# Rows gathered by DMA, counts in f16, integers read from low halves: one change to a two-layer encoder kernel

## The chip, the cores and the metric

The kernel runs on one core of a Trainium2 chip. The metric is the device time of a whole execution in microseconds. The kernel before takes 1705.83 us (median of 3 runs, 1701.89 to 1706.07).

The engines are called TensorE (PE in the profile, its weight loads PEld), VectorE (DVE), ScalarE (ACT), GpSimd (POOL) and SyncE (SP, which here only issues transfers).

## The reference

Input is x, 128 sequences of 64 rows of 128 numbers, and a context of the same shape. Each of the four layers adds its result to x:

```
x = x + corr_attention(layernorm(x), ctx)     # correlation by Fourier transform, 4 best shifts
x = x + ffn(layernorm(x))                     # rows quantised to 8 bit, ternary weights
x = x + cross_attention(ctx, layernorm(x))    # 16 heads of 64, a sequence's 64 rows of x ask 64 + 64 rows
x = x + experts(layernorm(x))                 # router: softmax, 2 of 8 experts a row
```

Of these, the change touches the quantisation in ffn, with `q = clip(round(x * scale), -128, 127)` before both of its products; the layer norm of both the context and the twice-normed x ahead of cross attention; the router's count of rows per expert; and the last sum, `output + y * combine_w`.

## The kernel before

The 8192 rows are 64 tiles of 128 (two sequences each), in 16 groups of 4. x stays in SBUF from the first load to the last store. The stages follow each other, with a barrier between: weights, a first loop (both layers of layer 0), cross attention with the router, the experts, the combination.

The first loop goes over the groups, software-pipelined five deep: one pass holds group g's correlation, g-1's shifts, g-2's statistics and quantisation, g-3's first product and activation, g-4's second product. The order on each engine is written out by hand in `step`. `quantise` (L531) scales rows and adds 12582912 (ROUND), which leaves the rounded integer in the f32's low bits, subtracts it again into a bf16 tile (L541), and TensorE turns that with an identity (`turn_rows`, L743). `quantise_hidden` (L582) does the same with the 512 hidden numbers a row (L589, L592), turned in `turn_hidden` (L837). ScalarE copies what was turned out of PSUM (L647, L675).

Cross attention takes steps; a chunk is 4 heads of one tile, 256 in all, and a tile is 4 steps. The offsets (`AT_S = 3`: a step works on the scores of the chunk three ahead) set which step of the pipeline an operation belongs to, and the order of the `if`s in each engine's `step` sets its place within it. Each tile is brought in by two transfers of the context (L992, L993), with statistics (L1088, L1089), a power of minus a half on GpSimd (L1011), the normalisation (L1100, L1101), and GpSimd's gains and offsets (L1015 to L1022). In the tile kv, half of the partitions take rows of x and the other half rows of the context, at two places n = 0, 1: so the normalisation runs on 64 partitions at a time. The output of a tile is added to x in L1063, after which TensorE may overwrite its bank (L1284).

The router goes over groups in the same steps: a group's parts stand at the steps in `ROUTE_...` (L966 to 969), 16 steps to a group. It writes each row twice as a pair of f16 parts (L1218 on ScalarE, L1031 on GpSimd) behind the number of the row (L1127), once per chosen expert, and scatters them by indirect DMA (L1042). `r_xn` and `r_rows` are single buffers: L1107 waits for the rests of the group before (`row_done`), L1218 and L1127 wait for its scatters. The rank of a row in its expert comes from five f32 products with a triangle and with ones (L1309 to 1312).

The experts read tiles of 256 rows, and scatter the results by the row number into `z`, choice by choice, tile by tile. The combination reads z in two transfers a group (L1511), with pieces of 512 bytes, does eight multiply-adds on VectorE (L1527) and stores from ScalarE's queue.

Of the kernel before, what the change touches and what calls it, by code (L numbers as in the profile page):

```python
# [35 lines left out]
def constants():  # L36
# [30 lines left out]
    out[:, C_DST:C_DST + 2 * TILES] = np.arange(2 * TILES)[None] * P + ch[:, None]  # L67
# [6 lines left out]
    out[0, C_N0:C_N0 + 8] = np.arange(8) * BATCH * SEQ  # L74
# [43 lines left out]
def load_weights(nc, s, dram):  # L118
# [148 lines left out]
def first_layer(nc, s, dram):  # L267
# [10 lines left out]
    with ExitStack() as ctx:  # L278
# [32 lines left out]
        xr = sb("b_xr", [P, GT, D])  # L311
        qb = [sb(f"b_q{n}", [P, GT, D], BF16) for n in range(2)]
# [12 lines left out]
        q2 = [sb(f"b_q2{n}", [P, GT, FF], BF16) for n in range(2)]  # L325
# [142 lines left out]
        def _(dve):  # L468
# [62 lines left out]
            def quantise(g, k):  # L531
# [50 lines left out]
            def quantise_hidden(g, k):  # L582
# [54 lines left out]
        def _(act):  # L637
# [28 lines left out]
            def step(i, k):  # L666
# [66 lines left out]
        def _(pe):  # L733
            wq, wk, wv, wo = (s.w_l0[:, n, :] for n in range(4))

            def turn_rows(i, k, g, p):
# [5 lines left out]
                for j in range(GT):  # L742
                    pe.transpose(QT[:, P * j:P * j + P], qb[p][:, j, :], s.ident_b[:])  # L743
# [860 lines left out]
```

## Time and profile before

| | us |
|---|---|
| median of the runs | 1705.83 |
| profiled execution | 1701.37 |
| its span | 1699.5 |
| TensorE busy | 1416.6 (83%) |
| VectorE busy | 1433.0 (84%) |
| ScalarE busy | 1256.2 (74%) |
| GpSimd busy | 1087.7 (64%) |

The busy times are of one profiled execution, and its span is the time from its first instruction to its last. A wait is the idle time of an engine ahead of an instruction, with the instruction that released it. A line's number is that of the kernel before.

### The profile page before, as it was taken

Reading aid. Unit: us, or ns where it says so; the run is one execution under the profiler, and the core shown is the slowest. Engines: PE = TensorE matmul, PEld = TensorE weight load, DVE = VectorE, ACT = ScalarE, POOL = GpSimd, SP = SyncE. Lnnn points to the kernel's source line nnn. Section 1 sums busy time; section 2 is a strip of 40 time slices with the busy share of each in tenths; the row PEclk is TensorE's granted clock in tenths of the full one; section 3 lists DMA queues with packets and bytes.
Section 4 is the critical chain, followed back from the end, with each engine's and each line's share of the span. In section 5 each row is a group of like instructions: output and inputs, shape, how many; then the busy total and the mean of one; then the engine's idle time right before and its main releaser. Section 6 shows DMA issues by size and latency. Waiting matters only on the chain. (4 is left out here: it accounts for less than half of the span.)

```text
span 1699.5 us, 53032 instructions
## 1 busy us (share of the span) xinstructions
PE 1416.6 (83%) x17149; PEld 1211.3 (71%) x17165; DVE 1433.0 (84%) x4161; ACT 1256.2 (74%) x3802; POOL 1087.7 (64%) x1498
## 2 busy tenths in 40 slices
PE   4788888873899999999999999999999937999960
PEld 3676676752788787788778778877877726888850
DVE  3579999985899999999999999999999835888868
ACT  1368877763899999888889888888988805666640
POOL 1367776653656677786777778777777564666650
PEclk8989999986999999999999999999999968999985
DMA  4445444200000000000000000000000003332219
GB/s 138 162 164 182 172 162 154 105 1 8 8 8 7 7 18 15 11 17 12 11 16 16 12 11 15 14 11 14 16 11 8 13 32 81 86 83 79 81 29 297
DMA packets 101785, 97.22 MB, mean 57 GB/s; under 512 B 13256, under 2 KB 87275, under 8 KB 101504
## 3 DMA queue, kind: packets, MB, share of 16 engines
q1 hardware_dynamic: 84544, 74.22, 13.7%
q0 software_dynamic: 8640, 16.87, 3.0%
q10 hardware_dynamic: 8448, 4.20, 0.8%
q8 instruction: 83, 1.36, 0.3%
q14 instruction: 70, 0.57, 0.1%
HBM read 39.32 MB, written 56.83 MB: 57 GB/s over the span
## 5 line engine op out<-in xcount | busy, mean ns | idle before, releaser
L1002 POOL TENSOR_TENSOR c_p<-c_p,c_rden 128x512 f32<-128x512 f32 x256 | 266.4, 1040 | 174.1 <-DVE c_rden L1067 172.1
L1207 ACT ACTIVATE c_p<-bank,c_nmax 128x128 f32<-128x128 f32 x1024 | 361.6, 375 | 4.7 <-DVE c_nmax L1053 4.6
L1207 ACT ACTIVATION_READ_ACCUMULATOR c_p<-bank,c_nmax 128x1 f32 x1024 | 221.6, 216 | 0.0
L1378 POOL DMA_INDIRECT moe_outputs<-e_y,e_rows x142 | 151.8, 1069 | 94.1 <-DVE e_y L1407 58.5
L1053 DVE TENSOR_REDUCE c_nmax<-bank 128x4 f32<-128x512 f32 x256 | 174.2, 681 | 38.1 <-PE bank L109 34.3
L107 PE MATMUL bank<-c_kvT,qk_fused 128*128 128x128 f16 x1024 | 187.6, 221 | 1.6 <-ACT c_kvT L1186 1.4
L108 PE MATMUL bank<-c_kvT,qk_fused 128*128 128x128 f16 x1024 | 187.5, 221 | 0.0
L109 PE MATMUL bank<-c_kvT,qk_fused 128*128 128x128 f16 x1024 | 187.5, 221 | 0.0
L1274 PE MATMUL bank<-const,c_p 128*128 128x128 f32 x1024 | 156.8, 276 | 13.3 <-DVE c_pT0rest L1078 12.4
L1446 ACT ACTIVATE e_h<-bank,moe_b 128x256 f32<-128x256 f32 x284 | 117.8, 465 | 65.0 <-PE bank L109 63.6
L1042 POOL DMA_INDIRECT moe_slots<-r_rows,r_pos x128 | 131.0, 1023 | 35.8 <-issue 35.8
L107 PE MATMUL bank<-vo_fused,c_o0high 128*128 128x128 f16 x512 | 93.2, 220 | 32.2 <-DVE x L1063 32.2
L1274 PEld LDWEIGHTS bank<-const,c_p 128*128 128x128 f32 x1024 | 108.3, 141 | 15.9 <-POOL c_p L1002 13.2
L107 PE MATMUL bank<-vo_fused,c_o1high 128*128 128x128 f16 x512 | 92.6, 220 | 19.5 <-DVE x L1063 19.5
L107 PEld LDWEIGHTS bank<-c_kvT,qk_fused 128*128 128x128 f16 x1024 | 103.4, 101 | 3.3 <-ACT c_kvT L1186 2.3
L1191 ACT ACTIVATE c_pT0high<-bank 128x512 f16<-128x512 f32 x128 | 76.7, 599 | 34.4 <-PE bank L1274 33.8
L108 PEld LDWEIGHTS bank<-c_kvT,qk_fused 128*128 128x128 f16 x1024 | 101.3, 99 | 0.4
L109 PEld LDWEIGHTS bank<-c_kvT,qk_fused 128*128 128x128 f16 x1024 | 101.3, 99 | 0.0
L107 PE MATMUL bank<-c_kvT,c_g0high 128*128 128x128 f16 x512 | 93.8, 221 | 1.4 <-DVE c_g0rest L1072 1.3
L1072 DVE SCALAR_TENSOR_TENSOR c_g0rest<-bank,c_g0high 128x512 f16<-128x512 f32 x128 | 84.9, 663 | 11.2 <-ACT c_g0high L1181 11.2
L108 PE MATMUL bank<-c_kvT,c_g0high 128*128 128x128 f16 x512 | 93.8, 221 | 0.0
L109 PE MATMUL bank<-c_kvT,c_g0rest 128*128 128x128 f16 x512 | 93.7, 221 | 0.0
(312 smaller groups left out, 6006.1 us busy)
## 6 DMA issues: line engine op xcount, KB each, us to landing
moe_slots<-slot_fill SPq DMA_DIRECT2D x66, 516.0 KB, 5.7
e_rows<-moe_slots SPq DMA_DIRECT2D x71, 129.0 KB, 2.2
f_z<-moe_outputs SPq DMA_DIRECT2D x32, 256.0 KB, 4.9
x<-in_x SPq DMA_DIRECT2D x16, 256.0 KB, 3.2
a_ctx<-in_ctx SPq DMA_DIRECT2D x32, 128.0 KB, 3.3
moe_stage<-in_L_ffn_W SPq DMA_DIRECT2D x16, 256.0 KB, 3.1
c_ctx<-in_ctx SPq DMA_DIRECT2D x128, 32.0 KB, 2.0
out_x<-x ACTq DMA_DIRECT2D x16, 256.0 KB, 4.8
```

Of the source, the lines that this page charges most:

```text
L107: pe.matmul(out, lhs[0], rhs[0], start=start, stop=False)
L108: pe.matmul(out, lhs[0], rhs[1], start=False, stop=False)
L109: return pe.matmul(out, lhs[1], rhs[0], start=False, stop=stop)
L1002: pool.tensor_tensor(pr[r % 4][:], pr[r % 4][:], rep(rden[r % 4][:], 2, P), ALU.mult).then_inc(m["pn"], 1)
L1042: pool.indirect_dma_start(s.xs, bass.IndirectOffsetOnAxis(ap=pos[:, c, j:j + 1], axis=0), rows[:, c, j, :], None).then_inc(scattered, 16)
L1053: dve.tensor_reduce(nmax[r % 4][:], SB[r % 2][:].rearrange("p (h c) -> p h c", h=4), AX.X, ALU.max, negate=True).then_inc(m["max"], 1)
L1072: dve.scalar_tensor_tensor(lo, GB[r % 2][:].rearrange("p (a n) -> p a n", a=2), 0.125, hi, ALU.mult, ALU.subtract).then_inc(m["g_copied"], 1)
L1191: act.activation(ptc[r % 2][0][:], PT[:], ACT.Copy).then_inc(m["pt_high"], 1)
L1207: last = act.activation(pr[r % 4][:, h, :], SB[r % 2][:, P * h:P * h + P], ACT.Exp, bias=nmax[r % 4][:, h:h + 1], accum_out=den[r % 4][:, ...
L1274: last = pe.transpose(PT[:, P * h:P * h + P], pr[r % 4][:, h, :], s.ident)
L1378: pool.indirect_dma_start(s.z, bass.IndirectOffsetOnAxis(ap=xr[t % XBUF][:, h, 2 * D:ROW].bitcast(U32), axis=0), ys[t % YBUF][:, h, :], No ...
L1446: act.activation(hf[t % 2][:, b, :], HB[b][:, 0:TSLOT], ACT.Gelu_apprx_tanh, bias=s.moe_b1[:, bass.ds(e * KB + b, 1)]).then_inc(m["gelu"], 1)
```

## The change

It has six parts.

1. First loop: ROUND_HALF = ROUND + 0x6600 is added instead of ROUND. The low 16 bits of the f32 are then, read as f16, the number 1536 + q. TensorE turns these halves at once (every second f16 of the f32 tile), and ScalarE takes 1536 off as it copies. The two subtractions on VectorE go. ScalarE's copy of 640 columns becomes two, since the last 128 are bf16 still.
2. Cross attention: a tile `c_rows` of two places takes the place of `c_ctx`. Four transfers a tile bring rows of the context from memory, and rows of x from SBUF, to the place and the half where the normalisation wants them; it then works on 128 partitions at a time. GpSimd does the epsilon in two operations with a drain between.
3. The addition of the output (L1063, L1072 after) goes to the head of VectorE's step, ahead of the maximum.
4. The router's mask, counts, triangle and ones are f16. Copies of rows, rests and row numbers move by one step.
5. The rows of z are numbered by partition first, then tile, then choice: a partition's results are then side by side.
6. Combination: two transfers a group, pieces of 2 KB. ScalarE scales the second choice, VectorE does four multiply-adds and one addition of 512.

```diff
-                for j in range(GT):
-                    dve.tensor_scalar(xr[:, j, :], xc[:, j, :], qs[:, j:j + 1], ROUND, ALU.mult, ALU.add)
-                dve.drain()
                 wait(dve, mb["qt"], g - 1)
-                dve.tensor_scalar(qb[k][:], xr[:], ROUND, None, ALU.subtract).then_inc(mb["q"], 1)
+                for j in range(GT):
+                    last = dve.tensor_scalar(xr[k][:, j, :], xc[:, j, :], qs[:, j:j + 1], ROUND_HALF, ALU.mult, ALU.add)
+                last.then_inc(mb["q"], 1)
...
-                    dve.tensor_scalar(ge[k][:, j, :], ge[k][:, j, :], qs2[:, j:j + 1], ROUND, ALU.mult, ALU.add)
-                dve.drain()
-                wait(dve, mb["q2t"], 2 * (g - 1))
-                dve.tensor_scalar(q2[k][:], ge[k][:], ROUND, None, ALU.subtract).then_inc(mb["q2"], 1)
+                    last = dve.tensor_scalar(ge[k][:, j, :], ge[k][:, j, :], qs2[:, j:j + 1], ROUND_HALF, ALU.mult, ALU.add)
+                last.then_inc(mb["q2"], 1)
...
+        def integers(ap, first):
+
+            return ap.bitcast(F16)[:, 2 * first:2 * (first + P):2]
...
-                        last = pe.transpose(T2[r][:, to:to + P], q2[p][:, 2 * r + j, P * b:P * b + P], s.ident_b[:])
+                        last = pe.transpose(T2[r][:, to:to + P], integers(ge[p][:, 2 * r + j, :], P * b), s.ident_h[:])
...
-                    act.activation(qt[b[1]][:], QT[:, 0:GT * P + P], ACT.Copy).then_inc(mb["qt_copied"], 1)
+                    act.activation(qt[b[1]][:, 0:GT * P], QT[:, 0:GT * P], ACT.Identity, bias=s.moffset[:])
+                    act.activation(qt[b[1]][:, GT * P:GT * P + P], PT[:, GT * P:GT * P + P], ACT.Copy).then_inc(mb["qt_copied"], 1)
...
-        ROUTE_HIGH, ROUTE_LOW, ROUTE_STEP, ROUTE_BASE, ROUTE_POS = 43, 44, 44, 46, 47
+        ROUTE_HIGH, ROUTE_LOW, ROUTE_STEP, ROUTE_BASE, ROUTE_POS = 44, 45, 45, 46, 47
...
-                sp.dma_start(cs[k][0:64, :], cvw[1, t, :, :]).then_inc(c_loaded[k], 16)
-                sp.dma_start(cs[k][64:128, :], cvw[0, t, :, :]).then_inc(c_loaded[k], 16)
+                for half in range(2):
+                    rows = slice(64 * half, 64 * half + 64)
+                    sp.dma_start(cs[k][rows, 1 - half, :], cvw[1 - half, t, :, :]).then_inc(c_loaded[k], 16)
+                    sp.dma_start(cs[k][rows, half, :], s.xg(i)[rows, k, :]).then_inc(c_loaded[k], 16)
...
-                    for half in range(2):
-                        rows = slice(64 * half, 64 * half + 64)
-                        dve.tensor_scalar(kv[r][rows, half, :], s.xg(g)[rows, r, :], a[rows, 0, 0:1], b[rows, 0:1], ALU.subtract, ALU.mult)
-                        last = dve.tensor_scalar(kv[r][rows, 1 - half, :], cs[r][rows, :], a[rows, 1, 0:1], b[rows, 1:2], ALU.subtract, ALU.mult)
+                    for n in range(2):
+                        last = dve.tensor_scalar(kv[r][:, n, :], cs[r][:, n, :], a[:, n, 0:1], b[:, n:n + 1], ALU.subtract, ALU.mult)
...
-    zv = s.z.rearrange("(k t p) d -> p k t d", k=2, p=P)
+    zv = s.z.rearrange("(p t k) d -> p t k d", k=2, p=P)
...
+                for j in range(GT):
+                    last = act.activation(share[g % 2][:, j, :], zt[g % 4][:, j, 1, :], ACT.Copy, scale=gate[:, GT * g + j, 1:2])
+                last.then_inc(m["scaled"], 1)
...
-                for k in range(2):
-                    for j in range(GT):
-                        last = dve.scalar_tensor_tensor(s.xg(g)[:, j, :], zt[q][:, k, j, :], gate[:, GT * g + j, k:k + 1], s.xg(g)[:, j, :], ALU.mult, ALU.add)
-                    if k == 0:
-                        dve.drain()
-                last.then_inc(m["combined"], 1)
+                for j in range(GT):
+                    dve.scalar_tensor_tensor(s.xg(g)[:, j, :], zt[g % 4][:, j, 0, :], gate[:, GT * g + j, 0:1], s.xg(g)[:, j, :], ALU.mult, ALU.add)
+                dve.drain()
+                dve.wait_ge(m["scaled"], g + 1)
+                dve.tensor_tensor(s.xg(g), s.xg(g), share[g % 2][:], ALU.add).then_inc(m["combined"], 1)
```

VectorE in the middle of one pass of the first loop, before and then after (`b_q` is the bf16 tile of integers, `b_gelu` the hidden numbers, in the second piece lines are numbered as in the changed kernel):

```order
L584 RECIPROCAL b_qs<-b_mx 128x4 [waits b_scale2]
L586 SCALAR_TENSOR_TENSOR b_qs<-b_qs,b_tmp 128x4
L589 TENSOR_SCALAR b_gelu<-b_gelu,b_qs 128x512 x4
L592 TENSOR_SCALAR b_q<-b_gelu 128x2048
L483 TENSOR_TENSOR a_prod<-bank,a_kk 128x512 [waits a_kk_copied]
L533 RECIPROCAL b_qs<-b_mx 128x4 [waits b_r1]
L535 SCALAR_TENSOR_TENSOR b_qs<-b_qs,b_rr 128x4
L538 TENSOR_SCALAR b_xr<-b_xc,b_qs 128x128 x4
L541 TENSOR_SCALAR b_q<-b_xr 128x512 [waits b_qt]
```

```order
L592 RECIPROCAL b_qs<-b_mx 128x4 [waits b_scale2]
L594 SCALAR_TENSOR_TENSOR b_qs<-b_qs,b_tmp 128x4
L597 TENSOR_SCALAR b_gelu<-b_gelu,b_qs 128x512 x4
L492 TENSOR_TENSOR a_prod<-bank,a_kk 128x512 [waits a_kk_copied]
L542 RECIPROCAL b_qs<-b_mx 128x4 [waits b_r1]
L544 SCALAR_TENSOR_TENSOR b_qs<-b_qs,b_rr 128x4
L548 TENSOR_SCALAR b_xr<-b_xc,b_qs 128x128 [waits b_qt]
L548 TENSOR_SCALAR b_xr<-b_xc,b_qs 128x128 x3
```

The two rows that write `b_q` are gone, and `a_prod` and everything behind it follow at once on the scaling.

VectorE in cross attention, from a normalisation (`c_kv`) to the statistics of the next tile, before and then after:

```order
L1100 TENSOR_SCALAR c_kv<-x,c_mv,c_rstd 64x128 [waits c_kv,c_rstd]
L1101 TENSOR_SCALAR c_kv<-c_ctx,c_mv,c_rstd 64x128
L1100 TENSOR_SCALAR c_kv<-x,c_mv,c_rstd 64x128
L1101 TENSOR_SCALAR c_kv<-c_ctx,c_mv,c_rstd 64x128
L1127 TENSOR_SCALAR r_rows<-r_rows 128x8 [waits r_scattered]
L1053 TENSOR_REDUCE c_nmax<-bank 128x4 [waits c_s]
L1063 TENSOR_TENSOR x<-x,bank 128x128 [waits c_w]
L1067 RECIPROCAL c_rden<-c_den 128x4 [waits c_exp]
L1072 SCALAR_TENSOR_TENSOR c_g0rest<-bank,c_g0high 128x2x256 [waits c_g_high]
L1078 TENSOR_TENSOR c_pT1rest<-bank,c_pT1high 128x512 [waits c_pt_high]
L1084 TENSOR_TENSOR c_o1rest<-bank,c_o1high 128x8x64 [waits c_o_high]
L1088 BN_STATS c_bn<-x 128x6 [waits c_ctx_loaded3]
```

```order
L1118 TENSOR_SCALAR c_kv<-c_rows,c_mv,c_rstd 128x128 [waits c_kv,c_rstd]
L1118 TENSOR_SCALAR c_kv<-c_rows,c_mv,c_rstd 128x128
L1072 TENSOR_TENSOR x<-x,bank 128x128 [waits c_w]
L1076 TENSOR_REDUCE c_nmax<-bank 128x4 [waits c_s]
L1086 RECIPROCAL c_rden<-c_den 128x4 [waits c_exp]
L1091 SCALAR_TENSOR_TENSOR c_g0rest<-bank,c_g0high 128x2x256 [waits c_g_high]
L1097 TENSOR_TENSOR c_pT1rest<-bank,c_pT1high 128x512 [waits c_pt_high]
L1103 TENSOR_TENSOR c_o1rest<-bank,c_o1high 128x8x64 [waits c_o_high]
L1108 BN_STATS c_bn<-c_rows 128x6 [waits c_ctx_loaded3]
```

The four rows of 64 partitions are two of 128. The addition to x (L1063) stood behind the maximum (`c_nmax`) and now stands ahead of it, and the row numbers (`r_rows`) have moved behind the statistics.

GpSimd around the rests of the router's rows (`r_rows<-r_xn`), where `c_p<-c_p,c_rden` is the first operation of each step, before and then after:

```order
L1031 TENSOR_TENSOR r_rows<-r_xn,r_rows 128x4x128 [waits r_row_high]
L1031 TENSOR_TENSOR r_rows<-r_xn,r_rows 128x4x128
L1002 TENSOR_TENSOR c_p<-c_p,c_rden 128x512 [waits c_rden]
L1015 TENSOR_TENSOR c_kv<-c_kv,ln_g 128x256 [waits c_kvn]
L102 ISA
L1018 TENSOR_TENSOR c_kv_parts<-c_kv,ln_b 128x256 [waits c_o]
L1020 TENSOR_TENSOR c_kv<-c_kv,ln_b 128x256
L1022 TENSOR_TENSOR c_kv_parts<-c_kv,c_kv_parts 128x256
L1002 TENSOR_TENSOR c_p<-c_p,c_rden 128x512 [waits c_rden]
```

```order
L1013 TENSOR_TENSOR c_p<-c_p,c_rden 128x512 [waits c_rden]
L1027 TENSOR_TENSOR c_kv<-c_kv,ln_g 128x256 [waits c_kvn]
L107 ISA
L1030 TENSOR_TENSOR c_kv_parts<-c_kv,ln_b 128x256 [waits c_o]
L1032 TENSOR_TENSOR c_kv<-c_kv,ln_b 128x256
L1034 TENSOR_TENSOR c_kv_parts<-c_kv,c_kv_parts 128x256
L1043 TENSOR_TENSOR r_rows<-r_xn,r_rows 128x4x128 [waits r_row_high]
L1043 TENSOR_TENSOR r_rows<-r_xn,r_rows 128x4x128
L1013 TENSOR_TENSOR c_p<-c_p,c_rden 128x512 [waits c_rden]
```

The rests stood in a step of their own, right behind a `c_p`; now they stand one step later, behind the four rows of `c_kv`.

## Rows read from the trace of the kernel before

**Rows 1.** Three stages: busy us per engine, granted clock, DMA share, GB/s.

```profile
85.00:412.00 327.00, 260.21 (x2353) 212.22 (x2369) 287.15 (x1101) 240.45 (x475) 215.38 (x398) 0.94 0.34 122
412.00:1392.00 980.00, 880.45 (x11634) 758.78 (x11633) 874.72 (x2410) 836.57 (x2930) 691.22 (x917) 0.97 0.04 13
1656.00:1699.50 43.50, 0.00 (x0) 0.00 (x0) 35.20 (x128) 0.00 (x0) 0.00 (x0) 0.50 0.99 290
```

**Rows 2.** Waits, 412 to 1392 us: total us, times, longest.

```profile
PE bank L107 <- DVE x L1063: 51.8, 61, 2.3
DVE c_nmax L1053 <- PE bank L109: 34.3, 60, 1.3
ACT r_rows L1218 <- DMA moe_slots<-r_rows,r_pos: 34.0, 14, 11.4
```

**Rows 3.** Combination, 1645 to 1700 us, and two windows with DMA rates.

```profile
L1527 DVE SCALAR_TENSOR_TENSOR x<-f_z,d_gate,x 128x128 f32<-128x128 f32 x128 | 35.2, 345 | 13.1 <-DMA f_z<-moe_outputs 11.8
...
75.00:80.00 5.00, 2.89 (x24) 2.51 (x22) 4.60 (x12) 1.67 (x3) 0.00 (x0) 1.00 1.04 404
1676.00:1680.00 4.00, 0.00 (x0) 0.00 (x0) 3.85 (x15) 0.00 (x0) 0.00 (x0) 0.50 1.15 345
```

**Rows 4.** Groups by shape, 100 to 340 us; the last row from the page.

```profile
L837 PE MATMUL bank<-ident_bf,b_q 128*128 128x128 bf16 x176 | 13.5, 220 | 12.5 <-DVE b_q L592 12.5
L592 DVE TENSOR_SCALAR b_q<-b_gelu 128x2048 bf16<-128x2048 f32 x11 | 13.5, 1227 | 1.2 <-issue 0.6
...
L541 DVE TENSOR_SCALAR b_q<-b_xr 128x512 bf16<-128x512 f32 x12 | 5.1, 427 | 0.9
...
L1274 PE MATMUL bank<-const,c_p 128*128 128x128 f32 x1024 | 156.8, 276 | 13.3 <-DVE c_pT0rest L1078 12.4
```

**Rows 5.** One group of the first loop in time, VectorE, then ScalarE.

```profile
226.06 0.69 DVE L483 TENSOR_TENSOR a_prod<-bank,a_kk 128x512 f32<-128x512 f32 x1
...
237.64 1.10 DVE L490 MAX8 a_top<-a_corr 128x8 f32<-128x64 f32 x8
...
240.39 0.17 DVE L494 TENSOR_TENSOR a_ev<-a_top 128x32 f32<-128x32 f32 x1
...
246.15 0.68 DVE L483 TENSOR_TENSOR a_prod<-bank,a_kk 128x512 f32<-128x512 f32 x1
...
235.16 0.60 ACT L719 ACTIVATE a_corr<-bank 128x512 f32<-128x512 f32 x1 [0.31 <-PE bank L809]
...
240.86 0.70 ACT L675 ACTIVATE b_qt<-bank 128x640 bf16<-128x640 bf16 x1
...
245.53 0.58 ACT L652 ACTIVATE a_kk<-bank 128x512 f32<-128x512 f32 x1
```

**Rows 6.** Groups by shape, 400 to 1360 us: busy us, mean ns, idle before.

```profile
L1207 ACT ACTIVATE c_p<-bank,c_nmax 128x128 f32<-128x128 f32 x1024 | 361.6, 375 | 4.7 <-DVE c_nmax L1053 4.6
...
L1101 DVE TENSOR_SCALAR c_kv<-c_ctx,c_mv,c_rstd 64x128 f32<-64x128 f32 x128 | 45.3, 354 | 0.0
...
L1100 DVE TENSOR_SCALAR c_kv<-x,c_mv,c_rstd 64x128 f32 x88 | 38.5, 437 | 0.7
...
L1100 DVE TENSOR_SCALAR c_kv<-x,c_mv,c_rstd 64x128 f32<-64x128 f32 x40 | 14.5, 363 | 6.0 <-POOL c_rstd L1011 5.7
```

**Rows 7.** VectorE in order of time, cross attention: start us, us, line.

```profile
823.98 0.98 DVE L1100 TENSOR_SCALAR c_kv<-x,c_mv,c_rstd 64x128 f32 x1
824.89 0.33 DVE L1101 TENSOR_SCALAR c_kv<-c_ctx,c_mv,c_rstd 64x128 f32<-64x128 f32 x1
...
831.76 1.54 DVE L1107 TENSOR_SCALAR r_xn<-x,r_mv,r_rstd 128x128 f32 x4
```

**Rows 8.** GpSimd in order of time, the steps of rows 7.

```profile
822.70 2.19 POOL L1031 TENSOR_TENSOR r_rows<-r_xn,r_rows 128x512 f16<-128x512 f32 x2
827.01 1.04 POOL L1002 TENSOR_TENSOR c_p<-c_p,c_rden 128x512 f32<-128x512 f32 x1 [2.13 <-DVE c_rden L1067]
...
830.78 0.68 POOL L1022 TENSOR_TENSOR c_kv_parts<-c_kv,c_kv_parts 128x256 f16<-128x256 f32 x1
```

More of the change, by code:

```diff
@@ L66, in constants @@
     out[:, C_ONE:C_ONE + P] = 1
-    out[:, C_DST:C_DST + 2 * TILES] = np.arange(2 * TILES)[None] * P + ch[:, None]
+    choice, tile = np.arange(2)[:, None], np.arange(TILES)[None, :]
+    out[:, C_DST:C_DST + 2 * TILES] = (2 * (ch[:, None, None] * TILES + tile) + choice).reshape(P, 2 * TILES)
     out[:, C_IT:C_IT + 72] = np.arange(72)[None]
@@ L73, in constants @@
         out[:, C_TILE + j] = ch // 32 == j
-    out[0, C_N0:C_N0 + 8] = np.arange(8) * BATCH * SEQ
+    out[:, C_N0:C_N0 + 8] = np.arange(8)[None] * (BATCH * SEQ // P)
     return out.astype(np.float32)
@@ L310, in first_layer @@
         xc = sb("b_xc", [P, GT, D])
-        xr = sb("b_xr", [P, GT, D])
-        qb = [sb(f"b_q{n}", [P, GT, D], BF16) for n in range(2)]
+        xr = [sb(f"b_xr{n}", [P, GT, D]) for n in range(2)]
         qt = [sb(f"b_qt{n}", [P, GT * P + P], BF16) for n in range(2)]
@@ L557, in bias_rows @@
             def bias_rows():
-                hi, mid, lo, all_ = (q2[0][:, n, :] for n in range(4))
+                hi, mid, lo, all_ = (ge[1][:, n // 2, :].bitcast(BF16)[:, n % 2 * FF:n % 2 * FF + FF] for n in range(4))
                 rest = ge[0][:, 0, :]
@@ L656, in gelu @@
                 if j == 0:
-                    wait(act, mb["q2"], g - 1)
+                    wait(act, mb["q2t"], 2 * (g - 1))
                 act.activation(ge[k][:, j, :], HB[j % 2][:], ACT.Gelu, scale=deq[k][:, j:j + 1]).then_inc(mb["gelu"], 1)
@@ L905, in cross_attention @@
         parts = lambda name, shape: [sb(name + part, shape, F16) for part in ("high", "rest")]
-        cs = [sb(f"c_ctx{n}", [P, D]) for n in range(4)]
+        cs = [sb(f"c_rows{n}", [P, 2, D]) for n in range(4)]
         kv = [sb(f"c_kv{n}", [P, 2, D]) for n in range(4)]
@@ L1007, in step @@
                     pool.wait_ge(m["stats"], v + 1)
-                    pool.tensor_tensor(b[:, 1:2], a[:, 1, 1:2], s.eps[:, 0:1], ALU.add)
-                    pool.tensor_scalar(b[:, 0:1], a[:, 0, 1:2], 1.0 + EPS, EPS * EPS, ALU.mult, ALU.add)
+                    pool.tensor_tensor(b[:], a[:, :, 1], norm_mul[:], ALU.mult)
+                    pool.drain()
+                    pool.tensor_tensor(b[:], b[:], norm_add[:], ALU.add)
                     pool.drain()
@@ L1043, in step @@
                                             rows[:, c, j, :], None).then_inc(scattered, 16)
+            for half in range(2):
+                rows_of = slice(64 * half, 64 * half + 64)
+                pool.memset(norm_mul[rows_of, half:half + 1], 1.0 + EPS)
+                pool.memset(norm_mul[rows_of, 1 - half:2 - half], 1.0)
+                pool.memset(norm_add[rows_of, half:half + 1], EPS * EPS)
+                pool.memset(norm_add[rows_of, 1 - half:2 - half], EPS)
+            pool.drain()
             walk(pool, FIRST, LAST, 16, LO, HI, step)
@@ L1049, in step @@
             def step(i, k):
+                if t := tile(i, k, AT_X3):
+                    v, r, g = t
+                    dve.wait_ge(m["w"], 4 * v + 4)
+                    dve.tensor_tensor(s.xg(g)[:, r, :], s.xg(g)[:, r, :], WB[:, 0:P], ALU.add).then_inc(m["x3"], 1)
                 if n := number(i, k, AT_S, CHUNKS):
@@ L1086, in step @@
                     v, r, g = t
-                    dve.wait_ge(c_loaded[r], 32 * (g + 1))
-                    dve.bn_stats(bst[:, 0, :], s.xg(g)[:, r, :])
-                    dve.bn_stats(bst[:, 1, :], cs[r][:])
+                    dve.wait_ge(c_loaded[r], 64 * (g + 1))
+                    for b in range(2):
+                        dve.bn_stats(bst[:, b, :], cs[r][:, b, :])
                     dve.drain()
@@ L1136, in step @@
                     dve.tensor_tensor(crun[:], crun[:], picked[:], ALU.add)
-            dve.tensor_scalar(dest, s.dst_rows.rearrange("p (k t) -> p k t", k=2)[:, :, 0:GT], float(-GT * P), None, ALU.add)
+            dve.tensor_scalar(dest, s.dst_rows.rearrange("p (k t) -> p k t", k=2)[:, :, 0:GT], float(-2 * GT), None, ALU.add)
             dve.tensor_copy(crun[:], s.count0)
+            dve.tensor_copy(tri[:], s.tri)
+            dve.tensor_copy(ones[:], s.ones)
             dve.memset(one8[:], 1.0)
@@ L1497, in combine @@
 def combine(nc, s, m, z_in, sb, gate, out):
-    zt = [sb(f"f_z{n}", [P, 2, GT, D]) for n in range(4)]
+    zt = [sb(f"f_z{n}", [P, GT, 2, D]) for n in range(4)]
+    share = [sb(f"f_share{n}", [P, GT, D]) for n in range(2)]
     ov = out.rearrange("(t two) s d -> (two s) t d", two=2)
-    zv = s.z.rearrange("(k t p) d -> p k t d", k=2, p=P)
+    zv = s.z.rearrange("(p t k) d -> p t k d", k=2, p=P)
     with nc.Block() as block:
```

56 lines of the change are left out of this document (32 added, 24 removed).

## The prediction

> **What bounds the kernel now.** I read the stages first, then who waits for whom in the longest stage, then the costliest groups of instructions by shape, then the order of time of single groups. The stages [rows 1]: the first loop runs from 85 to 412 us, cross attention with the router from 412 to 1392, the combination from 1656 to the end; the experts between are not touched but for where their results are written. In the first loop VectorE is busy 287 of 327 us, in cross attention 875 of 980, beside ScalarE 837 and TensorE 880. So VectorE leads narrowly, and what is taken from it is worth less than its length, since two engines stand 4 to 5% behind. The waits of cross attention [rows 2] say the same: TensorE idles 51.8 us for the addition of the output (L1063), VectorE 34.3 us for scores from TensorE, ScalarE 34.0 us for the router's scatters. In the combination VectorE issues without a gap: 3.85 of 4 us, while the DMA moves 345 GB/s [rows 3].
>
> **First loop.** Removed are one subtraction of 128x512 (427 ns) and one of 128x2048 (1227 ns) in each of 16 groups [rows 4]. With the overlap of neighbours (some 0.09 us) and the drains (0.08 us) that went with them, both go at their length: 1.65 us a group, 26 us in all. A group takes 246.15 - 226.06 = 20.1 us [rows 5], and VectorE works 287 of the stage's 327 us, so it is VectorE's own length that counts. Two things take some back. ScalarE's copy of 128x640 (0.70 us) becomes one of 128x512 and one of 128x128. It stands in a chain that starts at VectorE's L494 (ends 240.56) and ends with L652 (245.53 + 0.58 = 246.11), and VectorE's product starts at 246.15, without slack [rows 5]. The second copy costs between 0.1 (the difference in width) and 0.6 us (a whole copy); I take 0.3, near the small ScalarE operations, which is 4 us over 13 full groups. And ScalarE has its correlation ready at 235.76, where VectorE, which takes it at 237.64 and is 1.65 shorter by then, will want it at 235.99 [rows 5]: 0.2 us of slack are left, and for the groups that miss it I take 2 us in all. The bias in the three copies hides in that same idle time of ScalarE; without cover it would be 0.1 us each, 5 us. So the first loop gives **-20 us** (bounds -26 and -10).
> The transposes of the integers will read every second f16: 20 a group, 320 in all, 0.22 us each now, where an f32 transpose of the same size takes 0.276 [rows 4]. Strided reading costs between nothing and that difference, 0.056 x 320 = 18 us if all of it were on the path; I take nothing, because the elements still number 128, and TensorE waited 12.5 us in 12 groups for the operation that goes [rows 4], which covers most of it.
>
> **Cross attention, normalisation.** Each of 64 tiles now has four VectorE operations on 64 partitions, 38.5 + 14.5 + 45.3 = 98.3 us together [rows 6]. After there are two a tile on 128 partitions with as many elements each. I price them as L1101, 354 ns: 128 x 0.354 = 45.3 us. Saved are 53 us, less the overlap with the neighbour that also goes (824.96 - 824.89 = 0.07 us [rows 7], 128 times, 9 us): 44 us. By L1107 (1.54 us for four, beside GpSimd [rows 7]) the new ones would cost 0.385 each and 40 us would be saved; I go between, 42. ScalarE and TensorE are close behind, so I let three quarters count: **-31** (bounds -44 and -15).
> **The output added first.** TensorE's product for the next tile waits for L1063, 51.8 us over 64 tiles, 0.8 us a tile. L1063 now goes ahead of the maximum (0.68 us). TensorE gains up to 0.7 us a tile, 43 us, but TensorE isn't the bound; what VectorE can get is a part of its 34.3 us of waits for scores [rows 2]. I take a quarter: **-8** (0 to -25).
> **The router one step later.** Row copies (ScalarE), rests (GpSimd) and row numbers (VectorE) each move one step. ScalarE's wait for the scatters, 34.0 us in 14 groups with one of 11.4 at the end, mostly goes in the loop: of 34.0 - 11.4 = 22.6 I let two thirds go, 15 us of ScalarE, worth **-6** (0 to -15). But GpSimd's rests (2.19 us) land behind the four operations of the layer norm in the same step, and VectorE's L1107 waits for them. In the trace the step's first GpSimd multiplication starts at 827.01, the four end at 831.46, and L1107 starts at 831.76 [rows 7, 8]. With the rests behind 831.45 they end at 833.64, so VectorE would stand still for 1.9 us a group, 15 times, 28 us. VectorE has a few waits in that step which would absorb part, and after a stall it finds the others ahead: I take **+18** (bounds +5 and +30). Queued behind L1107 on VectorE are the maximum of the next step and all that ScalarE's exponentials need. GpSimd's next multiplication comes 2.2 us late too, but TensorE reads it two steps (7.4 us) later.
> A collision goes: L1100 took 0.98 us at 823.98 and ended at 824.96, just as GpSimd's rests (822.70 + 2.19 = 824.89) ended, against a mean of 437 and 363 ns [rows 6, 7, 8]. After the change the rests don't lie beside the normalisation: 0.6 us x 14, of which I count **-6**. By the Trainium skill (SBUF — State Buffer, Who interferes with whom) VectorE's two-port operations and GpSimd exclude each other for a whole instruction. The row agrees; by the rule L1107, released together with GpSimd's next multiplication, could lose up to 1.0 us to it once more, which would be 15 us, though its 1.54 us for four already hold such a collision.
> The counts in f16 turn five f32 products of a group into single-pass ones, on TensorE, which isn't the bound: **-2** (0 to -8). The square root's extra multiplication with a drain on GpSimd (0.3 us a tile) is hidden by the two steps until its reader. The rows of x gathered by DMA add 128 small transfers of 32 KB; VectorE waits only at the first tile, where the SP queue issues four transfers instead of two: **+1** (0 to +2).
> Cross attention: -31 - 8 - 6 + 18 - 6 - 2 + 1 = **-34 us**.
>
> **Combination.** A group has 8 VectorE operations, 35.2/16 = 2.2 us, 2.27 with the drain [rows 3]. After there are 4 of them (1.1 us), a drain and one addition of 128x512 (0.69 us by L483, of the same size [rows 5]): 1.9 us, 0.37 less, 16 times 5.9 us. ScalarE's four scalings, at most 0.375 each by its exponentials [rows 6], make 1.5 us and lie beside. A group moves 0.79 MB, which in 1.9 us is 414 GB/s; the DMA reached 404 in another window [rows 3], so it is at its end: **-4** (bounds 0 and -6).
>
> **The sum.** -20 - 34 - 4 = -58 us. The profiled execution took 1701.4 us (span 1699.5 and 1.9 around it), which is 4.4 below the median shown, 1705.8. So the changed kernel stands at 1643 by the one and 1648 by the other; I forecast **1648 us**.
>
> **Rivals.** *The freed time turns into waits.* If ScalarE and TensorE hold the pace of cross attention, VectorE's 42 us are worth a third, the reordering nothing, and the stall at L1107 counts in full: -14 - 6 + 28 = +8 there, -20 and -4 beside it, 1690. For it: ScalarE is at 85% and TensorE at 90% of the stage; against it: the waits of VectorE are only 4% of the stage. A milder form, half of the whole sum, gives 1677.
> *Everything counts.* VectorE's whole saving and no stall: -26 - 42 - 15 - 10 - 5 = -98, 1608. Against it: the chain through L652 has no slack now.
> *Slower: the results lie apart.* The expert results of a partition lie 64 KB apart from the next one's, where before neighbours of 512 bytes lay side by side. If the memory serves that badly, the combination is bound by it: it moves 12.6 MB (36.4 us at 345 GB/s), and the change comes out slower than before once the rate falls under 12.6 MB / (36.4 + 58 us) = 133 GB/s; at 115 GB/s it takes 110 us, 1648 + 74 = 1722. For it nothing in the trace; against it 2 KB pieces in place of 512 bytes, and one fast window.
> [...]
> *The integers aren't cheaper.* If strided reading costs TensorE the full f32 price in the chain, the first loop gives -2 instead of -20: 1666.
>
> **How the numbers follow.** Forecast 0.52 (1628 to 1668 by itself), waits in place of work 0.24 (1690, or 1677 in the milder form), everything 0.08, integers dear 0.08, slower through the memory 0.05, something else 0.03. About 0.3%, 5 us, is what a measurement of this kernel tells from none. Within 5 us of before falls only the worst end of the second case, 0.04; slower is the memory and half of the rest, 0.06; faster 0.90. The range 1614 to 1694 leaves out the slower case and the outer part of "everything".
>
> **What would show it.** Right: the first loop shorter by about 20 us and its groups at 18.7 us with a wait of VectorE for L652; cross attention at about 946 us; a wait of VectorE's L1107 for GpSimd's rests of 1 to 2 us a group; TensorE's wait for the addition at a third; the combination at 39 us with more than 360 GB/s. Wrong: no shorter group in the first loop (then TensorE or the strided reads bind), ScalarE's or TensorE's waits unchanged in length while VectorE's grow, or transfers of the results landing later than now.

## The result, and the profile after

The changed kernel takes 1645.6 us (median of 3, 1640.1 to 1647.7) against 1705.8: ratio 0.9643, interval 0.9628 to 0.9657. Forecast were 1648. The profiled execution took 1647.7, its span is 1645.9, 53.6 us less than before (1699.5). I cut both traces at the same instructions: start +1.7, first loop -19.3, cross attention with the router -30.6, experts -1.3, combination -4.1.

The three stages, to be read against [rows 1] (same columns; windows moved with the stage):

```profile
86.66:394.36 307.70, 262.19 (x2370) 211.21 (x2370) 265.07 (x1069) 244.31 (x491) 214.69 (x398) 0.93 0.36 130
394.36:1343.55 949.19, 867.79 (x11553) 751.60 (x11551) 829.22 (x2284) 827.79 (x2930) 695.76 (x925) 0.96 0.06 18
1606.48:1645.90 39.42, 0.00 (x0) 0.00 (x0) 28.63 (x80) 20.44 (x64) 0.00 (x0) 0.50 0.95 320
```

VectorE lost 22 us of work in the first loop and 45 in cross attention, where the stage got only 31 shorter: it is now busy 829 of 949 us, a smaller share (87%) than before (89%), so something else holds it as well.

The first loop: one group in time, VectorE and then ScalarE (start us, length us), against [rows 5].

```profile
222.60 0.68 DVE L492 TENSOR_TENSOR a_prod<-bank,a_kk 128x512 f32<-128x512 f32 x1
...
232.73 1.10 DVE L499 MAX8 a_top<-a_corr 128x8 f32<-128x64 f32 x8
...
235.48 0.17 DVE L503 TENSOR_TENSOR a_ev<-a_top 128x32 f32<-128x32 f32 x1
...
240.48 0.86 DVE L481 BATCH_NORM_STATS2 a_bn<-x 128x6 f32 x4
241.39 0.69 DVE L492 TENSOR_TENSOR a_prod<-bank,a_kk 128x512 f32<-128x512 f32 x1
```

```profile
235.96 0.69 ACT L681 ACTIVATE b_qt<-bank,minus_offset 128x512 bf16<-128x512 f16 x1
236.55 0.27 ACT L682 ACTIVATE b_qt<-bank 128x128 bf16<-128x128 bf16 x1
...
240.78 0.58 ACT L658 ACTIVATE a_kk<-bank 128x512 f32<-128x512 f32 x1
```

A group takes 241.39 - 222.60 = 18.79 us, 1.30 less, and so it is over ten groups (19.1 us against 20.4). The chain from L503 to L658 and on to L492 has no slack in this group (240.78 + 0.58 = 241.36): from the start of L503 to the end of L658 it takes 5.88 us, against 5.72 from L494 to L652 before, 0.16 more, which is what the two copies take beyond the one (235.96 to 236.82, 0.86 us, against 0.70). But VectorE's own work ends with it (240.48 + 0.86 = 241.34). Of the eleven groups from 143 to 336 us only four wait for that copy; in the other seven it was there 0.1 to 1.0 us before, and VectorE's own work sets the pace. The transposes that read every second f16, to be read against [rows 4]:

```profile
L844 PE MATMUL bank<-ident_f,b_gelu 128*128 128x128 f16 x176 | 13.5, 220 | 0.1
```

Same count, same 220 ns, and the wait of 12.5 us in front of them is gone: the stride costs TensorE nothing.

The waits of cross attention after (engine, tile, line, and what was waited for: total us, times, longest), against [rows 2]:

```profile
DVE c_nmax L1076 <- PE bank L114: 37.2, 59, 1.2
ACT c_p L1226 <- DVE c_nmax L1076: 36.9, 28, 2.5
PE bank L1293 <- DVE c_pT1rest L1097: 36.5, 17, 2.7
...
DVE r_xn L1124 <- POOL r_rows L1043: 21.5, 14, 3.6
ACT r_rows L1237 <- DMA moe_slots<-r_rows,r_pos: 19.3, 2, 11.3
...
PEld bank L112 <- DVE x L1072: 6.7, 20, 1.1
...
PE bank L112 <- DVE x L1072: 0.9, 1, 0.9
```

TensorE's wait for the addition is all but gone (its products 0.9 us against 51.8, where a third was forecast), and so is ScalarE's for the scatters in the loop: the two that are left come at 1324 us and later. The stall that was forecast is there, 1.5 us a group at VectorE's L1124 (L1107 before), and two waits that I had not in the sum stand behind it: ScalarE for the maximum (4.6 us before), TensorE for L1097 (0.9 us for L1078 before). One group in time, VectorE, GpSimd, ScalarE and TensorE:

```profile
742.05 0.68 DVE L1103 TENSOR_TENSOR c_o1rest<-bank,c_o1high 128x512 f16<-128x512 f32 x1
744.19 1.64 DVE L1124 TENSOR_SCALAR r_xn<-x,r_mv,r_rstd 128x128 f32 x4 [1.46 <-POOL r_rows L1043]
...
746.20 0.66 DVE L1076 TENSOR_REDUCE c_nmax<-bank 128x4 f32<-128x512 f32 x1
...
741.77 2.20 POOL L1043 TENSOR_TENSOR r_rows<-r_xn,r_rows 128x512 f16<-128x512 f32 x2
743.94 1.04 POOL L1013 TENSOR_TENSOR c_p<-c_p,c_rden 128x512 f32<-128x512 f32 x1
...
746.89 0.37 ACT L1226 ACTIVATE c_p<-bank,c_nmax 128x128 f32<-128x128 f32 x1 [2.50 <-DVE c_nmax L1076]
...
748.40 0.72 PE L1293 MATMUL bank<-const,c_p 128*128 128x128 f32 x4 [2.70 <-DVE c_pT1rest L1097]
```

And the same place in windows of 2 us (columns as in [rows 1]; the third number from the end is the granted clock, 1.00 is 2.4 GHz and 0.50 is 1.2):

```profile
744.00:746.00 2.00, 1.70 (x31) 1.52 (x28) 1.81 (x5) 0.39 (x1) 1.72 (x4) 1.00 0.00 0
746.00:748.00 2.00, 0.00 (x0) 0.00 (x0) 1.93 (x7) 1.10 (x7) 1.24 (x2) 1.00 0.00 0
748.00:750.00 2.00, 1.60 (x7) 0.88 (x8) 1.68 (x6) 1.49 (x5) 0.20 (x1) 0.70 0.00 0
750.00:752.00 2.00, 2.00 (x19) 1.81 (x17) 2.00 (x5) 1.57 (x8) 1.40 (x3) 0.50 0.00 0
752.00:754.00 2.00, 2.00 (x30) 1.92 (x29) 1.24 (x5) 1.50 (x5) 1.07 (x1) 0.95 0.00 0
```

TensorE does nothing for 2.70 us, its clock then drops to half, and it works at half speed until about 752 us. From 575 us on the clock falls in nine of 13 groups, each time for about 3.4 us; cut into stretches of 15 us, the stage is short of 15.0 us of full clock.

### The profile page after: what moved, and what is told of

Read it like the earlier page. It is cut to its first block and busy times, and to the rows that moved or that the text cites. A ratio compares the mean times of both kernels' runs of the same rounds, so it can differ in the third digit from the quotient of the medians.

```text
span 1645.9 us, 52961 instructions
## 1 busy us (share of the span) xinstructions
PE 1407.7 (86%) x17084; PEld 1202.6 (73%) x17084; DVE 1359.9 (83%) x3955; ACT 1271.9 (77%) x3882; POOL 1091.5 (66%) x1507
## 5 line engine op out<-in xcount | busy, mean ns | idle before, releaser
L1226 ACT ACTIVATE c_p<-bank,c_nmax 128x128 f32<-128x128 f32 x1024 | 365.8, 388 | 37.0 <-DVE c_nmax L1076 36.9
L1013 POOL TENSOR_TENSOR c_p<-c_p,c_rden 128x512 f32<-128x512 f32 x256 | 266.8, 1042 | 134.6 <-DVE c_rden L1086 131.8
L1226 ACT ACTIVATION_READ_ACCUMULATOR c_p<-bank,c_nmax 128x1 f32 x1024 | 232.2, 228 | 0.0
L112 PE MATMUL bank<-c_kvT,qk_fused 128*128 128x128 f16 x1024 | 189.9, 223 | 4.3 <-ACT c_kvT L1205 3.6
L113 PE MATMUL bank<-c_kvT,qk_fused 128*128 128x128 f16 x1024 | 189.6, 222 | 0.0
L114 PE MATMUL bank<-c_kvT,qk_fused 128*128 128x128 f16 x1024 | 189.3, 222 | 0.0
L114 PE MATMUL bank<-vo_fused,c_o0rest 128*128 128x128 f16 x512 | 96.7, 225 | 0.0
L113 PE MATMUL bank<-vo_fused,c_o0high 128*128 128x128 f16 x512 | 96.6, 225 | 0.0
L112 PE MATMUL bank<-vo_fused,c_o0high 128*128 128x128 f16 x512 | 96.5, 225 | 0.0
L112 PE MATMUL bank<-c_kvT,c_g1high 128*128 128x128 f16 x512 | 93.5, 221 | 0.0
L113 PE MATMUL bank<-c_kvT,c_g1high 128*128 128x128 f16 x512 | 93.3, 220 | 0.0
L114 PE MATMUL bank<-c_kvT,c_g1rest 128*128 128x128 f16 x512 | 93.1, 220 | 0.0
```

Of the source, the lines that this page charges most:

```text
L112: pe.matmul(out, lhs[0], rhs[0], start=start, stop=False)
L113: pe.matmul(out, lhs[0], rhs[1], start=False, stop=False)
L114: return pe.matmul(out, lhs[1], rhs[0], start=False, stop=stop)
L1013: pool.tensor_tensor(pr[r % 4][:], pr[r % 4][:], rep(rden[r % 4][:], 2, P), ALU.mult).then_inc(m["pn"], 1)
L1226: last = act.activation(pr[r % 4][:, h, :], SB[r % 2][:, P * h:P * h + P], ACT.Exp, bias=nmax[r % 4][:, h:h + 1], accum_out=den[r % 4][:, ...
```

## The experiments

The second and third sets of runs met a chip on which the experts took 57 to 75 us longer for every kernel traced there, before included by its time (1768.9 and 1784.2 us); there I go by the ratio to before and by the length of cross attention in each trace, from VectorE's first preparation for the router (L1154) to its last table (L1188). A fall is one of the stretches of 3.4 us, in the middle of the stage, in which TensorE's clock is granted at half.

| kernel | ratio to before | interval | cross attention us | clock missing us | falls |
|---|---|---|---|---|---|
| before | 1 | | 982.9 | 4.9 | 3 |
| changed | 0.9643 | 0.9628-0.9657 | 952.3 | 15.0 | 9 |
| changed, again | 0.9645 | 0.9628-0.9662 | 949.3 | 13.2 | 8 |
| changed, third | 0.9691 | 0.9634-0.9747 | 965.5 | 18.4 | 11 |
| rests first | 0.9532 | 0.9516-0.9549 | 931.1 | 0 | 0 |
| router back | 0.9527 | 0.9510-0.9544 | 931.4 | 0 | 0 |
| addition behind | 0.9692 | 0.9677-0.9708 | 959.6 | 18.3 | 11 |
| first loop alone | 0.9875 | 0.9818-0.9933 | | | |
| norm in halves | 0.9837 | 0.9791-0.9883 | 977.2 | 10.0 | 6 |
| f32 counts | 0.9564 | 0.9517-0.9611 | 939.9 | 0 | 0 |
| f32 counts, again | 0.9527 | 0.9478-0.9575 | 939.9 | 0 | 0 |
| rests first, f32 | 0.9506 | 0.9445-0.9567 | 933.7 | 0 | 0 |
| rests first, spread | 0.9537 | 0.9485-0.9589 | 931.9 | 0 | 0 |
| results in 512 bytes | 0.9732 | 0.9675-0.9790 | 965.2 | 20.1 | 12 |

(Clock missing: the sum over stretches of 15 us from 435 to 1290 us of 15 x (1 - granted clock).)

**The base.** 

> The changed kernel once more, beside the kernels that it is compared with. Expected 0.964 of the time before, some 1645 us.

1644.9 us, as expected.

**The rests ahead of the layer norm.**

```diff
+                if (g := group(i, k, ROUTE_LOW)) is not None:      # moved here, unchanged
                 if t := tile(i, k, AT_KV):
...
-                if (g := group(i, k, ROUTE_LOW)) is not None:
```

> GpSimd's rests of the router's rows (L1043) go ahead of the four operations of the layer norm in the same step; nothing else is changed. Theory: VectorE's stall at L1124 (21.5 us in 14 groups) is on the path and pushes the maximum behind it, for which ScalarE then waits (36.9 us). Without it the wait at L1124 falls under 3 us, ScalarE's wait for the maximum to half, and cross attention gets 12 to 22 us shorter: 1623 to 1633 us. Rival: the stall is made good by work that stands ready behind it; then the wait goes and the time stays within 3 us of the changed kernel. Second rival: the layer norm, 2.2 us later on GpSimd, makes TensorE wait for the rows; then L1265's wait grows by 1 us or more a group and the time does not fall.

1626.7 us, 18.3 less than the changed kernel beside it. The stall is gone in the loop (one wait of 3.6 us at the start is left), and with it the falls of the clock. ScalarE's wait for the maximum fell by a third, not to half. The two rivals are out: L1265's only wait stays at 11.7 us.

**The router's rows back.**

```diff
-        ROUTE_HIGH, ROUTE_LOW, ROUTE_STEP, ROUTE_BASE, ROUTE_POS = 44, 45, 45, 46, 47
+        ROUTE_HIGH, ROUTE_LOW, ROUTE_STEP, ROUTE_BASE, ROUTE_POS = 43, 44, 44, 46, 47
```

> The router's row copies, rests and row numbers stand one step earlier again (43, 44, 44), the rest as in the changed kernel. Theory, by the terms forecast: the stall at L1124 goes (-18), the wait of ScalarE for the scatters (13 waits, 22.6 us before) comes back (+6), and the collision of GpSimd's rests with a normalisation (+6): 6 us less than the changed kernel, some 1639 us. Rival: the later step was worth more than its stall, since a waiting ScalarE holds everything; then the time is 8 us or more above the changed kernel.

1626.3 us, 18.6 less, where 6 were expected. Its waits in cross attention, and its normalisation:

```profile
ACT r_rows L1237 <- DMA moe_slots<-r_rows,r_pos: 35.0, 14, 11.3
...
ACT c_p L1226 <- DVE c_nmax L1076: 10.6, 16, 0.8
```

```profile
L1118 DVE TENSOR_SCALAR c_kv<-c_rows,c_mv,c_rstd 128x128 f32<-128x128 f32 x128 | 58.1, 494 | 5.5 <-POOL c_rstd L1023 5.5
```

and those of the version with the rests first:

```profile
ACT c_p L1226 <- DVE c_nmax L1076: 25.7, 26, 1.7
...
ACT r_rows L1237 <- DMA moe_slots<-r_rows,r_pos: 19.6, 2, 11.5
```

ScalarE waits 35.0 + 10.6 = 45.6 us in the one and 25.7 + 19.6 = 45.3 in the other. The wait for the scatters did not cost; taken away, it turned up as a wait for VectorE.

The collision of GpSimd's rests with the normalisation is real too: 494 ns a piece, against 374 in the changed kernel run beside it, 15 us in all. But these runs can't price it. With the rests first, L1124 meets GpSimd instead, and VectorE spends as long on the normalisation and L1124 together in either version: 58.1 + 22.3 = 80.4 us here, 47.9 + 32.7 = 80.6 with the rests first, against 42.6 + 25.1 = 67.7 in the changed kernel. Both versions took the stall away and brought 13 us of collisions back.

**The addition behind the maximum.** The four lines of L1072 go back to where L1063 was. 

> The addition of the output stands behind the maximum again, the rest as in the changed kernel. Theory: TensorE waits for it again, 30 to 50 us in all, and the time grows by 8 us (4 to 15): 1653 us. Rival: TensorE isn't the bound and ScalarE, which now waits 36.9 us for the maximum, gets it 0.2 us a tile earlier; then the time stays or falls by up to 5 us though TensorE's wait comes back.

1653.8 us, 8.9 more. The sum's term was 8. TensorE waits for the addition again, 31.8 us in its weight loads and 6.8 in its products, and the rival, no change or a gain, is out. A part of the 8.9 us is clock, since it falls in 11 groups here and in 8 of the changed kernel beside it.

**The first loop alone,** in the kernel before. 

> The kernel before with the first loop of the changed kernel and nothing else of it. Theory: the two operations go at their length less what ScalarE's chain gives back, 1.3 us a group (the changed kernel's group took 241.39 - 222.60 = 18.79 us, against 20.09): -20 us, some 1686 us, cross attention, experts and combination as before. Rival: the first loop's gain seen in the changed kernel comes in part from elsewhere, or is lost in the next stage, which starts earlier; then the time stays above 1692 us.

Ratio 0.9875 (0.9818 to 0.9933), which on 1706 us is -21 (-31 to -11). It agrees and can't say more: the rival, above 1692 us, is only just inside the interval. Its traced execution, 1773 us, is one of the three longest of eight (1747 to 1775), so I take nothing from its trace.

**The normalisation in halves.**

```diff
-                    for n in range(2):
-                        last = dve.tensor_scalar(kv[r][:, n, :], cs[r][:, n, :], a[:, n, 0:1], b[:, n:n + 1], ALU.subtract, ALU.mult)
+                    for half in range(2):
+                        rows = slice(64 * half, 64 * half + 64)
...                      # two operations on these 64 rows
```

> The changed kernel with the normalisation by four operations on 64 partitions again, its inputs gathered by DMA as now. VectorE gets 128 operations more; by the means of the rows 50 to 56 us of work. Theory as forecast: three quarters of 42 us count, so 31 us above the changed kernel (15 to 44), 1676 us. Rival: ScalarE, which now waits 36.9 us for VectorE's maximum, was not that close behind, and all of it counts: 42 us or more above. Second rival: what was gained came from the stall's neighbours; under 15 us.

Against the changed kernel's 0.9645 and 0.9691 it is 1.5 to 1.9% of 1706, 25 to 33 us; with the intervals it is some 12 to 41 us. The theory holds and the first rival is out. The second, under 15 us, is unlikely but not out: cross attention took 977.2 us, 25 and 28 more than in the changed kernel's first two traces, but only 12 more than in its third, where the clock fell 11 times and not 6.

**The counts in f32.**

```diff
-        mask = sb("r_mask", [P, GT, EXPERTS], F16)
+        mask = sb("r_mask", [P, GT, EXPERTS])
...
-        tri, ones = sb("r_tri", [P, P], F16), sb("r_ones", [P, P], F16)
+        tri, ones = s.tri, s.ones
...                      # and the running count, in f32 too
```

> The changed kernel with the router's masks and counts in f32 again. Theory: TensorE gets about 1.5 us of work a group more, of which little is on the path: 0 to 4 us above the changed kernel, 1647 us. Rival: the ranks stand between the mask and VectorE's positions with no slack; then 8 us or more.

Neither of the two: cross attention took 939.9 us, 9 to 12 less than the changed kernel in its first two traces, though VectorE stands still as before (20.7 us in 14 waits). At the place shown above, TensorE now does this (its wait, then the clock around it):

```profile
745.83 0.63 PE L1291 MATMUL bank<-const,c_p 128*128 128x128 f32 x4 [1.75 <-DVE c_pT1rest L1097]
```

```profile
743.00:745.00 2.00, 1.08 (x20) 0.91 (x17) 1.93 (x8) 0.67 (x4) 1.20 (x2) 1.00 0.00 0
745.00:747.00 2.00, 1.17 (x8) 0.73 (x9) 1.69 (x6) 1.75 (x8) 0.63 (x1) 1.00 0.00 0
747.00:749.00 2.00, 2.00 (x37) 2.00 (x36) 1.99 (x5) 1.97 (x9) 1.13 (x2) 1.00 0.00 0
```

The longer products fill TensorE just ahead of the stall, it idles 1.75 us instead of 2.70, and the clock stays. So I ran it again beside the changed kernel, and both edits together. 

> The changed kernel beside the next three. In its trace TensorE idles 2.70 us once in most groups of cross attention (until VectorE's L1097 behind the stall), and the clock granted to it is 0.70 and 0.50 in the 4 us behind that. Expected 0.9645 of the time before.

> The f32 counts once more, now beside the changed kernel. In the first run cross attention took 939.9 us against 949 to 952, and no stretch of 15 us of it had a clock under 1.00 from 420 us on. Theory from that: the f32 products fill 1 us a group of TensorE beside the stall, its longest idle time is 1.8 us in place of 2.7, the clock stays at its full level, and this is worth 8 to 12 us, more than the products cost: 1634 us, ratio to before 0.958. Rival: the first run's gain was a disturbance; then the time is 0 to 4 us above the changed kernel.

> The rests ahead of the layer norm and the f32 counts together. Theory: the two gains are the same one in part, since without the stall no clock is lost; then f32 counts are worth nothing on top or cost up to 4 us: 1626 to 1631 us, ratio 0.953 to 0.956. Rival: the gains are independent and add, -18 and -10: 1617 us, ratio 0.948.

The changed kernel came to 0.9691 here, with the expected 0.9645 inside its interval, the f32 counts to 0.9527, and both edits together to 0.9506, where 0.953 to 0.956 was expected and the rival's 0.948 can't be told from it; its trace (933.7 us) stands with the theory.

The intervals of the changed kernel (0.9634 to 0.9747) and of the f32 counts (0.9478 to 0.9575) don't meet, and the stage is 939.9 us both times: the disturbance is out. Of the four combinations, by cross attention: stall and f16 949 to 966, stall and f32 939.9, no stall and f32 933.7, no stall and f16 931.1. So the stall alone costs 6.2 us and f16 alone gains 2.6, but the two together cost 18 to 34. The gains are the same one in part, as expected; whole times can't tell the last two from each other.

That the rest is clock can be read inside one trace. These are three groups of the changed kernel, each from one L1124 to the next (columns as in [rows 1]), and TensorE's long wait in each:

```profile
801.50:858.90 57.40, 54.41 (x726) 47.53 (x723) 51.53 (x143) 51.71 (x184) 44.24 (x59) 0.97 0.06 18
858.90:914.70 55.80, 52.80 (x725) 45.71 (x722) 51.99 (x143) 51.39 (x184) 44.28 (x59) 1.00 0.06 19
914.70:972.10 57.40, 54.40 (x725) 47.09 (x723) 51.50 (x143) 51.67 (x184) 44.22 (x59) 0.97 0.06 18
```

```profile
805.71 0.63 PE L1293 MATMUL bank<-const,c_p 128*128 128x128 f32 x4 [2.69 <-DVE c_pT1rest L1097]
...
863.06 0.63 PE L1293 MATMUL bank<-const,c_p 128*128 128x128 f32 x4 [2.70 <-DVE c_pT1rest L1097]
...
918.88 0.63 PE L1293 MATMUL bank<-const,c_p 128*128 128x128 f32 x4 [2.70 <-DVE c_pT1rest L1097]
```

The code, the stall and the idle time are the same in all three. Where the clock fell, the group took 57.4 us, and where it did not, 55.8. From 687 to 1256 us this trace has seven groups of the first kind (57.1 to 57.4 us) and three of the second; in the same part of the stage every group takes 55.7 to 55.9 us with f32 counts, and 55.3 or 55.4 with the rests first. A fall costs 1.5 us, then, and the nine of them some 14; the stall without a fall costs 0.5 us a group. In the third trace a fall costs more, 2.2 us (58.1 us on average against 55.9); why stays open.

**The router's scalings spread over four steps,** with the rests first.

```diff
-                    for j in range(GT):
-                        last = dve.tensor_scalar(r_xn[:, j, :], ...
+                for j in range(GT):
+                    if (g := group(i, k, ROUTE_XN + j)) is not None:
```

> A version meant to beat both: GpSimd's rests ahead of the layer norm, and VectorE's four router scalings (L1124, 1.3 to 2.4 us in one step, behind which ScalarE waits 25.7 us for the maximum) spread over four steps, one in each. Theory: ScalarE's wait for the maximum falls to a third or less and 5 to 12 us go: 1615 to 1622 us. Rival: VectorE is the bound over the whole of a tile, and an order of the same work gives nothing: within 3 us of 1626.7 us. Second rival: the single scalings meet GpSimd's operations at more places, and each collision adds: slower than 1627 us.

Nothing: 931.9 us against 931.1. ScalarE's wait for the maximum fell from 25.7 to 19.1, VectorE's for scores rose from 19.6 to 29.4. The first rival holds, by the traces; the whole times (0.9485 to 0.9589) can't tell.

**Results in 512-byte pieces.**

```diff
-    zv = s.z.rearrange("(p t k) d -> p t k d", k=2, p=P)
+    zv = s.z.rearrange("(k t p) d -> p t k d", k=2, p=P)
...                      # the row numbers, and two transfers a group, one for each choice
```

> The changed kernel with the expert results stored and read as before (pieces of 512 bytes, neighbours side by side), while VectorE and ScalarE combine as in the changed kernel. Theory: the combination is set by VectorE's operations, 1.9 us a group, and the DMA can deliver in either form: the combination takes 35 to 36 us, as in the changed kernel (35.2 us), and the time is within 3 us of it. Rival: the rate above 346 GB/s (it reached 393) comes from the longer pieces; then the combination takes 38 us or more.

As a whole 0.9732 (0.9675 to 0.9790), some 7 us above the changed kernel beside it, which the intervals can't tell from none. By the stage the rival holds: from the first L1557 (L1556 there) to the end 38.8 us, against 35.8 in the changed kernel run beside it. The rates in the middle of it, of this kernel and of the changed one (its first trace; the one run beside it reaches 383 too):

```profile
1720.00:1730.00 10.00, 0.00 (x0) 0.00 (x0) 8.07 (x24) 5.90 (x19) 0.00 (x0) 0.50 1.15 345
```

```profile
1630.00:1640.00 10.00, 0.00 (x0) 0.00 (x0) 8.53 (x24) 5.81 (x19) 0.00 (x0) 0.50 1.09 383
```

## Why the prediction was right, and where not

- **First loop,** -20: measured -19.3 in the trace and -21 alone. The group came to 18.79 us (18.7 forecast), and the integers cost TensorE nothing, as taken. The second copy cost 0.16 us, for which I took 0.3, and VectorE waits 2.1 us in eight groups for ScalarE's correlation (L726), for which I took 2. Less right is the chain through L652: it holds four groups of eleven, and VectorE's own work the rest.
- **Normalisation,** -31: 25 to 33 by undoing it. VectorE saved 98.3 - 41.8 = 56.5 us where I took 42, and about half of it counted where I took three quarters: two errors that cancel.
- **The addition first,** -8: 8.9, of which a part is clock.
- **The stall,** +18: gone, it gave 18.3. The size is right and half of the reason is missing. VectorE's standing still costs 6 us, a third of the term, since VectorE makes most of it good; the rest is TensorE's clock, which fell behind an idle time of 2.70 us in most groups. I had looked at who waits behind L1107 and not at how long TensorE would idle in one piece. That the number came out is luck. (The 13 us of collisions that came back in this version are in the 18.3, so the stall may be worth somewhat more.)
- **Counts in f16,** -2: the step that failed. That it runs "on TensorE, which isn't the bound" is right where there is no stall (-2.6). In this kernel f16 costs 9 us or more, because TensorE then idles 2.70 us in one piece and not 1.75, and the clock falls 8 to 11 times instead of never.
- **Scatter wait,** -6: nothing. Router back and rests first differ by 15 us of it and by 0.3 us of time. It was read as a cost from a row that shows only a length; ScalarE waited the same 45 us in both.
- **Collision,** -6: the 15 us of VectorE's time did go, but what they are worth stays open, since the versions that undo this step or the stall bring most of them back elsewhere.
- **Rows gathered by DMA,** +1: nothing. The first maximum comes 17.8 us into the stage, against 17.9 before.
- **Combination,** -4: measured -4.1, for another reason in part. I took VectorE's issue for the bound and the layout for a risk. With the old pieces the new operations bring the stage to 38.8 us, next to the 39.25 of before: 345 GB/s with a DMA share of 1.15 [rows 3] was the limit of that layout, which VectorE's busy 3.85 of 4 us hid. That the new layout would give as little without the new operations is argued from that row and was not run. The Trainium skill (DMA: Bandwidth & Descriptors, Specifications) puts the full rate at 512 bytes and above. Here pieces of 512 bytes stay at 345 and pieces of 2 KB reach 383, so the measurement decides against it for this read. The two layouts also differ in which rows are neighbours, and no run changes the length of the pieces alone.
- The sum came out within 3 us because the misses cancel. In cross attention I had 41 us for normalisation, addition and counts together; the traces give 51.5 (982.9 to 931.4 us, router back). Against that, the 12 us for scatters and collision can't be found, and the stall with all that comes with it took 20.9 (931.4 to 952.3) and not 18. The 51.5 us are more than the parts undone one at a time (28, 9 and 2.6), since the clock falls in some versions and not in others. An estimate without the falls, from the lengths of groups with and without one in each trace (1.4 us a fall before, 1.5 in the changed kernel, 1.0 with the addition behind, 0.4 with the norm in halves), gives 36 to 38, 10 and 3 us for the three, together some 50, against 47 for the whole.
- **What beats both:** the changed kernel with the rests first, or with the router's steps as before, at 1626.7 and 1626.3 us, 0.953 of the kernel before. f32 counts or spread scalings add nothing that can be measured.

By the Trainium skill (SBUF — State Buffer, Who interferes with whom) L1107 could collide with GpSimd's next multiplication. Of its four scalings the one beside L1013 takes 0.87 us, the others 0.33, in the groups looked at: 0.54 us a group, the rule agrees, inside the bound of 1.0 that I gave.

## What to carry to other kernels

Beside the question who waits behind a stall, ask how long TensorE is idle in one piece there: a stall of 1.5 us on VectorE cost 18 us in 14 groups, two thirds of it through the clock, and making TensorE's work shorter at that place made the kernel slower. A version that undoes a step must be looked at for what else it brings back: here a collision moved from one line to another and could not be priced. A wait of an engine that runs ahead is no cost until something behind it is shown late; sum all waits of that engine before pricing one. When a stage shows an engine at 96% and a DMA rate that stays on one number, expect little from changing the engine's work alone: here it gave 0.4 us of 4.

## What I had not expected of the hardware

- Behind one idle time of TensorE of 2.6 to 2.7 us its clock fell to half for 3.4 us in 25 of 36 groups, in the three traces of the changed kernel. The length of that one idle time doesn't decide it: behind 1.95 us, at 575 us, it fell in all three, in the kernel before it fell in three of 12 groups behind 1.8 to 1.9 us, with the norm in halves in six of 13 behind 2.8 us, and with the rests first (1.7 to 1.8 us) or with f32 counts (1.7 to 1.75 us) never.
- Which groups fall varies from execution to execution: 13.2, 15.0 and 18.4 us of clock were missing in three traces of one kernel, and cross attention took 949.3, 952.3 and 965.5 us with it. A fourth trace with the same cross attention (results in 512 bytes) has 12 falls and 965.2 us.
- Pieces of 512 bytes, with neighbours side by side, held the DMA at 345 GB/s with steady numbers; pieces of 2 KB let it reach 383.
